# Output projections with the gate multiplied into their weights: 13 products on GpSimd in place of 40 products and 40 adds

## The reference

```
x = x + gate_a * (attn(norm(x)) @ W_so + b_so)
x = x + gate_c * (cross(norm(x), context) @ W_co + b_co)
x = x + gate_m * (mlp(norm(x)))
```

## Time and profile before

| | |
|---|---|
| median of 3 executions | 2871.01 us (2868.69 to 2883.15) |
| profiled execution | 2869.71 us |
| its span, first to last instruction | 2868.4 us |
| mean granted TensorE clock | 0.912 |
| PE busy | 2420.5 us (84%) |
| DVE busy | 1745.0 us (61%) |
| ACT busy | 1264.1 us (44%) |
| POOL busy | 375.5 us (13%) |

### The profile page before, as it was taken

One profiled execution on the slowest core, in us unless ns is written; L12 is line 12 of the kernel. 1 busy time (PEld: TensorE's weight loads), 2 busy tenths in 40 slices (PEclk: granted clock), 3 DMA queues, 4 the chain that ended last, 5 costly groups with the idle time before them and its releaser, 6 DMA issues.

```text
span 2868.4 us, 37341 instructions
## 1 busy us (share of the span) xinstructions
PE 2420.5 (84%) x13127; PEld 1239.4 (43%) x13127; DVE 1745.0 (61%) x5419; ACT 1264.1 (44%) x2410; POOL 375.5 (13%) x380
## 2 busy tenths in 40 slices
PE   6768677968997979999979999978889978899668
PEld 2455344544554544554434445432324332234335
DVE  5646856666234565557767666657676677775343
ACT  2324434433221314445525555525656626656334
POOL 3002333244010100000200010010010010010201
PEclk9889688989898979999989999989999989999879
DMA  4646231000000120000411100123110122110120
GB/s 157 170 118 201 89 114 32 17 24 6 3 8 30 67 61 12 12 23 26 143 59 57 36 16 23 45 88 98 50 32 12 67 81 75 31 26 8 55 60 15
DMA packets 151647, 161.32 MB, mean 56 GB/s; under 512 B 33471, under 2 KB 120978, under 8 KB 151196
## 3 DMA queue, kind: packets, MB, share of 16 engines
q1 hardware_dynamic: 151460, 158.94, 19.2%
HBM read 98.04 MB, written 60.19 MB: 55 GB/s over the span
## 4 chain that ended last, share of the span: by engine, by line
PE 62%; DVE 16%; issue 6%; ACT 5%; DMA 5%; POOL 4%; SPq 2%; POOLq 0%; ACTq 0%; DVEq 0%
PE bank L1125 9%; PE bank L1608 8%; PE bank L1097 7%; PE bank L1072 7%; PE bank L1629 5%; PE bank L736 3%; PE bank L1101 3%; PE bank L2082 3%; DVE max L1198 3%; DVE bank L1195 2%; PE bank L1528 2%; PE bank L2259 2%; PE bank L2084 1%; PE bank L676 1%; ACT work L1139 1%
## 5 line engine op out<-in xcount | busy, mean ns | idle before, releaser
L1139 ACT ACTIVATE work<-bank 128x512 f32<-128x512 f32 (+1 forms) x1216 | 700.7, 597 | 574.6 <-PE bank L1101 259.4
L1195 DVE CUSTOM_DVE_ANT_0 bank<-bank,weights 128x512 f32<-128x512 f32 x512 | 348.8, 703 | 197.8 <-PE bank L1072 196.4
L1198 DVE TENSOR_REDUCE max<-bank 128x1 f32<-128x512 f32 x512 | 341.3, 685 | 142.4 <-PE bank L1072 140.4
L1072 PE MATMUL bank<-k_stack,q_stack 97*128 97x512 bf16 x896 | 364.4, 410 | 70.5 <-DVE max L1198 28.6
L1097 PE MATMUL bank<-q_stack,k_stack 99*128 99x512 bf16 x896 | 345.4, 388 | 12.8 <-ACT work L1139 10.3
L1608 PE MATMUL bank<-hT,weights 128*128 128x512 f32 x512 | 268.3, 624 | 16.0 <-ACT hT L697 7.4
L1453 POOL TENSOR_TENSOR x<-x,work 128x512 f32<-128x512 f32 x64 | 82.1, 1282 | 1081.3 <-DVE work L1442 1076.9
L1101 PEld LDWEIGHTS bank<-ident_b,weights 128*128 128x128 bf16 x2048 | 159.3, 98 | 119.3 <-issue 10.3
L1072 PEld LDWEIGHTS bank<-k_stack,q_stack 97*128 97x128 bf16 x896 | 90.1, 101 | 267.8 <-DVE max L1198 99.3
L1101 PE MATMUL bank<-ident_b,weights 128*128 128x128 bf16 x2048 | 200.1, 220 | 0.0
L1629 PE MATMUL bank<-weights,work 128*128 128x256 f32 x768 | 196.5, 384 | 0.0
(11 more groups left out here) (237 smaller groups left out, 3687.2 us busy)
## 6 DMA issues: line engine op xcount, KB each, us to landing
q_stack<-parts_q SPq DMA_DIRECT2D x60, 384.0 KB, 3.9
parts_q<-parts SPq DMA_DIRECT2D x46, 384.0 KB, 2.6
k_stack<-parts_k SPq DMA_DIRECT2D x40, 384.0 KB, 4.8
weights<-parts_q SPq DMA_DIRECT2D x36, 384.0 KB, 3.7
parts_q<-parts SPq DMA_DIRECT2D x46, 256.0 KB, 2.9
parts_k<-parts SPq DMA_DIRECT2D x24, 384.0 KB, 2.5
parts_k<-parts SPq DMA_DIRECT2D x24, 256.0 KB, 2.9
weights<-in_L_e_w SPq DMA_DIRECT2D x12, 512.0 KB, 5.8
```

Of the source, the lines that this page charges most:

```text
L1072: m = pe.e.matmul(bank.ap[:, :], self.q(g)[0:MAX_ROW, h, qt * P:(qt + 1) * P], k_stacks[self.key, g].ap[0:MAX_ROW, h, half * BLK:(half + 1 ...
L1139: ac.e.activation(p.ap[0:self.nk, :], banks[self.key, "exp", g, i].ap[0:self.nk, :], ACT.Exp).then_inc(*probs.tick((self.key, g, i)))
L1195: ve.e.tensor_tensor_reduce(bank[:, :], bank[:, :], mask_bias[:, qt, half * BLK:(half + 1) * BLK], 1.0, -3.4e38, ALU.add, ALU.max, to).the ...
L1198: ve.e.tensor_reduce(to, bank[:, :], AX_X, ALU.max).then_inc(*maxima.tick((self.key, g, i)))
```

## The change

Two new buffers `gated` of the size of one projection's weights (128 x 2 x 256) are kept, one for each r. At the start of a gated `OutProject`, GpSimd waits for the weights, the rows and the last reader of the buffer, and writes weights times gate row into it, one instruction of 128x512. TensorE waits for this and multiplies with `gated` in place of the weights. VectorE adds the bank to x itself, after it has waited for the bias in x (or, without a bias, for the norm's reading). The multiplication at L1442 and the add at L1453 remain for the MLP only. The bias row is still multiplied with the gate and added on GpSimd. `rows_left` now names the gated product for the gate row, `added` the add on VectorE.

```diff
+        gated = slots([sb(f"gated{i}", [P, CC, C]) for i in range(2)])
...
             def added(self, t):
-                return (pool_done if self.gate is not None else vec)[self.key, "x", t - t % 2]
+                return (vec if self.direct else pool_done)[self.key, "x", t - t % 2]
...
                 if self.gate is not None:
-                    left.append((vec, (self.key, "y", self.tiles[-1] - 1)))
+                    left.append((pool_done, (self.key, "gated")) if self.direct else (vec, (self.key, "y", self.tiles[-1] - 1)))
...
-                if self.gate is None:
+                if self.direct:
                     if self.bias is not None:
                         ve.wait_ge(*pool_done[self.key, "pre", tp + 1])
+                    else:
+                        ve.wait_ge(*vec[self.norm.key, "z", tp + 1])
                     ve.e.tensor_tensor(x[b][:, tp:tp + 2, :], x[b][:, tp:tp + 2, :], src, ALU.add).then_inc(*vec.tick((self.key, "x", tp)))
...
         class OutProject(Adding):
+            direct = True
...
             def pool(self, po):
+                if self.gate is not None:
+                    w = gated.take(self.r, self.key, (dense, (self.key, "all")))
+                    for f in w.free:
+                        po.wait_ge(*f)
+                    po.wait_ge(*ld_w[self.wname][self.wname])
+                    po.wait_ge(*ld_tm[self.r][self.key, "rows"])
+                    po.wait_ge(*pool_done.latest)
+                    po.e.tensor_tensor(w.ap[:, :, :], wt[self.wname][:, :, :], tmc[self.r][:, 0:1, :].to_broadcast([P, CC, C]),
+                                       ALU.mult).then_inc(*pool_done.tick((self.key, "gated")))
                 self.pre_add(po)
                 yield
-                for what, tp, i in self.steps:
-                    yield
-                    if what == "pair" and i == 1 and self.gate is not None:
-                        self.add_pool(po, tp, work[self.key, "y", tp])
...
             def project(self, pe, bank, tile, i):
                 w = wt[self.wname]
+                if self.gate is not None:
+                    w = gated[self.key].ap
+                    pe.wait_ge(*pool_done[self.key, "gated"])
...
         class Mlp(Adding):
+            direct = False
```

More of the change, by code:

```diff
@@ L1512, in tensor @@
                             bank = banks.take(self.lane.banks[n % len(self.lane.banks)], k, (vec, (self.key, "y", at)))
-                            work.take(self.lane.work[4 + n % 4], (self.key, "y", at), (pool_done, (self.key, "x", at))
-                                      ) if self.gate is not None else None
                             for f in bank.free:
@@ L1520, in tensor @@
                             m.then_inc(*dense.tick(k))
+                            dense.also((self.key, "all"), k)
                             n += 1
@@ L1550, in vector @@
                         ve.wait_ge(*dense[self.key, tp])
-                        self.add_vector(ve, tp, banks[self.key, tp], work[self.key, "y", tp] if self.gate is not None else None)
+                        self.add_vector(ve, tp, banks[self.key, tp], None)
                     yield
         class Mlp(Adding):
+            direct = False
             def __init__(self, lane, b, name, norm, gated_unit, gate, bias, row_free, blk=None, r=None):
```

## The result

The changed kernel takes 2893.7 us (median of six runs, 2887.4 to 2900.2) against 2870.5 for the kernel before; the ratio is 1.0068, with a 95% interval of 1.0051 to 1.0086. That is 19.5 us (14.6 to 24.7) on 2871, slower by over 0.5%; the two medians alone lie 23.2 apart. Forecast were 2888.2 and a range of 2872 to 2902. The profiled execution took 2887.35 us (span 2885.9), against the 2886.9 of the sum; it was the fastest of the six, so that this comes within half a microsecond is chance.

What follows compares the result with a forecast made beforehand. TensorE's in-order stream, busy 84% of the span, was taken as the bound. Terms A to F sum to 18.7, less 1.5 gives +17.2 us: 2886.9 on the profiled execution, 2888.2 on the median, range 2872 to 2902.

Steps and rivals of the forecast that it cites:

- A: Cross attention of batch 0, second block: gated weights ready at 616.2 against 615.79 on TensorE; +0.4 us (0 to 1).
- C: Cross attention of batch 1, second block: weights ready at 811.3 against 809.24, TensorE working without a break; +2.0 us (1 to 2).
- the 1.5 for shorter ways: Places without a stall: shorter ways into x take some 1.5 us off the sum of 18.7.
- D: Self-attention of L2, batch 1: late row, TensorE stands 7.6 us, work done ahead now comes behind; +4.2 us (2 to 6).
- E: Self-attention of L3, batch 0: late row, TensorE stands 6.3 us, low-clock start possible; +4.2 us (2 to 6).
- VectorE and GpSimd exchange for nothing: Multiplications become adds on VectorE, 0.1 us; GpSimd saves 34 us, worth nothing by themselves.
- B: Cross attention of batch 1, first block: product behind GpSimd's memsets, TensorE stands 10.8 us; +3.5 us (0 to 10.8).
- F: Last phase, both halves of batch 1: second product starts 1.27 us later, 7 of 8 tiles wait; +4.4 us (2 to 6).
- 1, stalls hidden: Stalls hidden, mainly at D and E where VectorE bounds the scores: 2879 us, not slower; chance 0.32.
- 2, GpSimd makes room: Removed GpSimd adds had held up VectorE's two-port or two-input operations: 2846 us, faster; chance 0.05.
- 3, the clock: Low clock after pauses costs 9 us more at each of D, E and F: 2915 us; chance 0.15.
- 4: The change does not do what it says, leaving 2871 us; chance 0.01.

Runs made afterwards that it cites:

- e2: The kernel before with the change only at the seven blocks of places A to F: 2892.4 us, ratio 1.0065.
- e3: The changed kernel with the gate rows of D and E loaded one phase earlier on SP's queue: 2879.8 us, ratio 1.0027 to the kernel before.
- e6: The kernel before with the change at place B alone: ratio 1.0021, +6.0 us (2.0 to 10.0).
- e10: The kernel before with the change only at L0so of both batches and L0co of batch 0, block 0: ratio 1.0003, +0.9 us.
- e8: The kernel before with the change only at L2so of batch 0 and L2co of both batches: ratio 1.0018, +5.2 us.
- e1: The kernel before with the change only at the six projections without a TensorE wait for GpSimd: 2878.3 us, ratio 1.0025.
- e4: The changed kernel with ten products instead of thirteen, issued in earlier stages, and gate rows of D, E, F early: 2866.7 us, ratio 0.9976 to before.
- e9: e4 with the new form kept only at the seven blocks of A to F, the other six projections back to the old: 2863.6 us, 0.9970 to before.
- e5: The changed kernel with every product computed twice on GpSimd: 2902.8 us, ratio 1.0118 to the kernel before.
- e7: The kernel before with the change at place F alone, both blocks: ratio 1.0015, +4.3 us (0.3 to 8.6).

## Why the prediction was right, point by point

**The sum.** +17.2 forecast, +19.5 (14.6 to 24.7) measured; from the places in the changed kernel's own trace 0.3 + 3.0 + 0.5 + 7.4 + 3.4 + 4.9, again 19.5, with A taken at what it has over an unchanged kernel. That this agrees to the tenth is chance: the two traces end 17.5 apart, and in stretches that hold none of the places their difference falls by 4.6 us once and grows by 2 to 3 elsewhere. The forecast, too, owes some of its closeness to errors that cancel: C was too high by 1.2 to 1.5, the 1.5 for shorter ways did not show, and D and E were too low in the traces.

**The signs.** The products were to end at about 712, 1902, 2317 and 2692 us. Less what the traces already differed just ahead of each, they ended at 712.5, 1902.2, 2317.7 and 2692.0. TensorE's idle time grew by 19.9 us, well over the 8 under which the forecast would have failed.

**VectorE and GpSimd exchange for nothing.** Right: 687 against 692 ns, 34.0 us off GpSimd without a gain. The product's 1.27, taken from the add's row, measured 1.26.

**A and C.** A 0.4: 0.3 to 0.5. C 2.0: the wait was 2.11, but only 0.5 to 0.8 was left behind it in the changed kernel and in e2 (2.5 in e3). The step that failed is "TensorE works without a break there": ten microseconds later TensorE waits for VectorE's scaled tiles, and behind that wait its pace differs (timeline of TensorE, before):

```profile
823.01 0.67 PE L676 MATMUL bank<-ident,work 128*128 128x128 f32 x4 [2.93 <-DVE work L654]
...
824.88 1.92 PE L2084 MATMUL bank<-work,weights 77*128 77x512 f32 x2
```

and after:

```profile
831.19 0.67 PE L677 MATMUL bank<-ident,work 128*128 128x128 f32 x4 [2.40 <-DVE work L655]
...
832.78 1.02 PE L2101 MATMUL bank<-work,weights 77*128 77x512 f32 x2
```

The wait is 0.5 us shorter, and behind it the clock stayed at 1.00, where the kernel before had lost 1.2 us (0.57 from 824 to 828 us). In e3 the clock was 0.52 from 835.7 to 838.7 us, which fits the 2.5 that C costs there. So most of what C got back is the clock's doing, and not to be counted on.

**B.** TensorE stood 11.67 (10.8 worked out), the path grew by 2.8 to 3.1 in the traces of the changed kernel, e2 and e6 (3.5 forecast), 6.0 (2.0 to 10.0) in time. VectorE's statistics started 4.6 us later than the traces already differed, where the low clock was to give 4.5. Following VectorE's stream and not TensorE's stand gave the right size.

**D and E.** The mechanism was right. The sizes, 4.2 each, look low: 6.6 (2.0 to 10.9) and 6.3 (2.6 to 10.0) measured alone, 5.5 and 6.3 by TensorE's stream in the two traces, 4.6 and 5.5 by the means over all traces. The times alone do not exclude 4.2. The term that was mis-sized is the restart. At D "this work now comes behind: +4.2" counted the work at full clock; the half pace added 2.1, of which the kernel before had lost 1.2 in its own restart, so 0.9 on balance, and the row came 0.5 later. At E up to 1.7 was allowed for the low clock and it took 2.5, the row came 0.7 later, and "VectorE then bounds the scores and takes some of it back" took off 0.9 of 5.1, where up to the next norm only 0.2 came back; TensorE stood 7.58 there, not 6.3.

**F.** 4.4 forecast, 4.3 (0.3 to 8.6) alone. The second product did start one product length later and hold back 28 of 32 matmuls. In the two traces the last statistics end 4.9 us later, for the 5.1 of full length and low clock together.

**The 1.5 us from shorter ways** did not come: VectorE's statistics waited 10.6 us for GpSimd's adds and now wait 1.2, yet e10 (+0.9, -2.9 to 4.3) and e8 (+5.2) are not shown faster than before. The one shorter way found is the half microsecond at C. No run shows the term.

**The idle time named as a wait for GpSimd** was put at 25 to 32 us and is 37.5: A to E stood 29.8, for which the steps had 27.1; F stood twice, 7.7 together, of which the bound had left room for 5. So the forecast bound was missed here, without a cost in the sum, which did not go by it.

**The rivals.** 1, stalls hidden, fell: D, E and F alone cost 17.2 together, where less than 6 would have decided for it. 2, GpSimd makes room, fell: no kernel with the exchange alone (e1, e10, e8) is faster. The rule behind it (the Trainium skill, GPSIMD Engine Reference, Key points, on SBUF interfaces shared with VectorE) is not refuted by that, since the operations that stood beside these adds were not held up before either. In the trace before only one operation of VectorE took 0.1 us more than its median beside an L1453: L2281 at 805.42, which reads two tensors in SBUF, 1.38 us for 0.69. That add is the MLP's and stays, and in the changed kernel the same operation took 1.38 again. 3, the clock, was half right: the half pace behind a stand is there, about 2 us at D, 2.5 at E and 2.4 at B, but inside the terms and not 9 us at each of three places. The mean granted clock over the changed kernel's six runs is 0.9077; for before it is 0.9107 over the 29 runs of e1's group, which are not those that the changed kernel was compared with. The profiled run of the changed kernel has 0.913 and a time 6 us under the median, so the traces may show less of the clock than the times hold. 4 fell with the first row.

## What to carry to other kernels

Folding a row into the weights moves a deadline: the row must be there when the first matmul starts, and not when the first bank is evacuated. The product itself costs 1.26 us of GpSimd. What counts is what stands ahead of it on the in-order queues; placed early, with its row loaded a phase ahead, it costs nothing that shows, and e4 and e9 beat the kernel before by 0.24% and 0.30%. The early rows are enough for all of that gain: the stretches at D and E are 4.9 and 3.0 us shorter than before's, together 7.9, where e4 gained 6.9 (3.7 to 10.3) and e9 8.6 (4.0 to 13.5). So nothing shows that folding the gate into the weights gains anything by itself. Whether the early rows would give as much with the old form is not shown; the old form with early rows was not tried.

## What the runs showed of the hardware

After a stand of 7.6 to 8.1 us TensorE came back at the lower clock: 0.50 over the first 4 us, groups of four matmuls at 2.04 us for 1.03. After the 4.37 at F and the 4.27 at C in e5 the same 2.05 and 2.04. In e3 at D, where it had stood only 2.33 us for the stack's load, the groups took 1.03 at once. But the length of a stand does not settle it between 2.4 and 3.5 us. Behind the wait for the stack's load, the first group took 1.91 us after 2.44, 2.45 and 2.68 us (e1, e6, e7) and 1.03 after 2.39 and 2.62 us (e10, e8); after 2.9 us at E it took 1.03 in the kernel before and 1.91 in e6; and after 3.48 us at D the kernel before ran one microsecond at 1.00 and only then at 0.50. This is a good part of the scatter of a profile. After longer stands TensorE was not slow for longer: behind 9.1 and 10.0 us (D and E in e5) the clock was 0.62 over 4 us, behind 13.0 (B) 0.50. So a long wait is to be priced as its length less what was idle anyway, plus the restart (here 2.1 us at D and 2.5 at E), less what the kernel before lost in its own restart at the same place (here 1.2 and 0).

A product's span on GpSimd can be taken at its word here. In e5 the first of two products (L1497) and the second (L1500):

```profile
1914.15 1.26 POOL L1497 TENSOR_TENSOR gated<-weights,row_consts 128x512 f32<-128x512 f32 x1 [11.66 <-DMA row_consts<-mod_rows_L]
1915.49 1.26 POOL L1500 TENSOR_TENSOR gated<-weights,row_consts 128x512 f32<-128x512 f32 x1
```

The second waits for the first. The starts are 1.34 us apart, 0.08 more than the span, and in the changed kernel TensorE starts 0.15 us behind the end at D (1903.34 + 1.26, then 1904.75). The Trainium skill, Perfetto Trace Analysis, GPSIMD Engine Instruction, calls such spans unreliable and advises the spacing of starts. For this operation the two agree within 0.1 us.
